# A four-layer network of attention and mixtures on one core: 24 blocks of 32 gathered slots in place of dense experts

## The reference, cut to what matters

```python
logits = einsum('btc,ce->bte', x, Wg)
probs = softmax(logits)
top_vals, top_idx = top_k(probs, 2)
gates = (one_hot(top_idx, E) * top_vals[..., None]).sum(-2)
h = relu(einsum('btc,ech->bteh', x, W1) + b1)
y = einsum('bteh,ehc->btec', h, W2) + b2
out = einsum('bte,btec->btc', gates, y)
```

## Time and profile before

| | |
|---|---|
| median of 3 runs | 462.35 us (462.15 to 462.73) |
| span of the profiled execution | 461.0 us |
| PE busy | 438.0 us, 95% |
| DVE busy | 333.3 us, 72% |
| ACT busy | 232.7 us, 50% |
| POOL busy | 139.9 us, 30% |
| moved by DMA | 62.38 MB |

### The profile page before, as it was taken

One profiled execution on the slowest core, in us unless ns is written; L12 is line 12 of the kernel. 1 busy time (PEld: TensorE's weight loads), 2 busy tenths in 40 slices (PEclk: granted clock), 3 DMA queues, 4 the chain that ended last, 5 costly groups with the idle time before them and its releaser, 6 DMA issues.

```text
span 461.0 us, 9333 instructions
## 1 busy us (share of the span) xinstructions
PE 438.0 (95%) x3240; PEld 380.5 (83%) x3240; DVE 333.3 (72%) x756; ACT 232.7 (50%) x596; POOL 139.9 (30%) x178
## 2 busy tenths in 40 slices
PE   8999999999999999999999978899899999999997
PEld 7776999997676899998577756657699999879997
DVE  3775989995576989996475486511698999787774
ACT  1494455641295765642295275232284656365452
POOL 6012556561011465652001101200445665400000
PEclk9999999999999999999999999999999999999999
DMA  5560264710480155620389606005053756326650
GB/s 161 203 204 2 77 227 138 214 64 2 155 297 2 70 183 177 202 89 1 105 231 297 154 1 175 33 20 222 0 173 135 222 158 217 121 71 191 195 202 19
DMA packets 19365, 62.38 MB, mean 135 GB/s; under 512 B 4041, under 2 KB 6914, under 8 KB 19330
## 3 DMA queue, kind: packets, MB, share of 16 engines
q1 hardware_dynamic: 19330, 61.93, 42.5%
HBM read 59.82 MB, written 2.10 MB: 134 GB/s over the span
## 4 chain that ended last, share of the span: by engine, by line
PE 68%; issue 15%; ACT 6%; DVE 5%; POOL 3%; DMA 2%; POOLq 0%; SPq 0%; DVEq 0%
PE bank L1056 24%; PE bank L1064 10%; PE bank L1076 7%; ACT probs L574 5%; PE bank L724 4%; PE bank L1078 3%; PE bank L847 3%; PE bank L874 2%; PE bank L761 2%; DMA w<-in_M_w_dram 2%; PE bank L756 1%; PE bank L890 1%; POOL rstd L415 1%; PE bank L793 1%; PE bank L737 1%
## 5 line engine op out<-in xcount | busy, mean ns | idle before, releaser
L1056 PE MATMUL bank<-xT_hi,w_hi 128*128 128x256 f32 x408 | 109.2, 289 | 1.6 <-issue 1.6
L1363 DVE TENSOR_TENSOR w_lo<-w,w_hi 128x512 fp32r<-128x512 f32 x102 | 96.7, 987 | 2.3 <-ACT w_hi L613 0.4
L661 ACT ACTIVATE hid<-bank,b 128x256 f32<-128x256 f32 x150 | 62.7, 471 | 68.9 <-PE bank L1056 68.7
L1056 PE MATMUL bank<-xT_hi,w_lo 128*128 128x256 f32 x408 | 82.0, 282 | 0.0
L1056 PEld LDWEIGHTS bank<-xT_hi,w_hi 128*128 128x128 f32 x408 | 77.9, 191 | 3.9 <-issue 3.8
L471 POOL TENSOR_TENSOR w_hl<-w,consts 128x384 fp32r<-128x384 f32 x50 | 52.6, 1052 | 73.5 <-PE bank L1078 69.8
L1056 PEld LDWEIGHTS bank<-xT_hi,w_lo 128*128 128x128 f32 x408 | 63.4, 191 | 0.0
L473 POOL TENSOR_TENSOR w_hl<-w,w_hl 128x384 fp32r<-128x384 f32 x50 | 58.9, 1178 | 3.9
L1064 PE MATMUL bank<-w,hid 128*128 128x192 f32 x308 | 56.4, 327 | 2.3 <-issue 2.3
L613 ACT ACTIVATE w_hi<-w 128x512 fp32r<-128x512 f32 x102 | 58.3, 627 | 0.2 <-DMA w<-in_M_w_dram 0.2
L1056 PE MATMUL bank<-xT_lo,w_hi 128*128 128x256 f32 x204 | 57.7, 283 | 0.0
(11 more groups left out here) (178 smaller groups left out, 658.9 us busy)
## 6 DMA issues: line engine op xcount, KB each, us to landing
w<-in_M_w_dram SPq DMA_DIRECT2D x34, 768.0 KB, 5.5
w<-in_M_w_dram SPq DMA_DIRECT2D x33, 576.0 KB, 4.9
w<-in_M_w_dram SPq DMA_DIRECT2D x9, 288.0 KB, 2.8
wqkv<-in_A_wqkv_dram SPq DMA_DIRECT2D x4, 432.0 KB, 6.6
rel_scratch<-relall SPq DMA_DIRECT2D x4, 372.0 KB, 2.3
wproj<-in_A_wproj_dram SPq DMA_DIRECT2D x4, 288.0 KB, 7.4
wqkv<-in_M_w_dram SPq DMA_DIRECT2D x2, 576.0 KB, 21.1
rel<-rel_scratch SPq DMA_DIRECT2D x10, 96.0 KB
```

The costliest lines, as they stand in the source:

```text
L661: ins = act.activation(hid[:, 2 * b + c, :], bank[B_H[b]][:, c * T:(c + 1) * T], FUNC[cfg["act"]], bias=b1[:, kb, bass.ds(at, 1)])
L1056: ins = pe.matmul(bank[B_H[b]][:, c2 * T:(c2 + 1) * T], w, xs, start=(q == 0), stop=(q == 4))
L1363: dve.tensor_tensor(w1_cols(w1_lo, b), w1_cols(w1[s], b), w1_cols(w1_hi, b).bitcast(F32), ALU.subtract)\
```

## The change

**Gathering in the open mixtures.** M0, M1, M3 and M4 now gather too, in 24 blocks of 32 slots, and the four blocks of a group are four column tiles of 32. Each expert has one block of its own for its first 32 token-expert pairs: eight static blocks, two groups. What is beyond that fills 16 dynamic blocks, four groups. With 512 pairs in all, 16 blocks are enough for every routing. Which expert a dynamic block belongs to is counted on the chip (`owner`, from the number of pairs per expert). All eight experts' weights lie in SBUF (`rw1`, `rw2`). The weights of a dynamic block are copied from there to one of four tiles (`sw1`, `sw2`), at an address that depends on a register into which the expert's number was loaded (`value_load`). Tile 0 is copied by ScalarE, tile 1 by GpSimd, tiles 2 and 3 by VectorE. There is one set of tiles: w1 of the next group can be written when `up` has read the last, w2 when `down` has.

**Full precision.** The products of the experts are plain 32-bit products; the parts, and the instructions that make them, are gone. The bias b1 is a further row of w1 (K = 128 + 65). The shared experts of M3 and M4 are two further groups, ahead of the static ones, over the 128 tokens of each half. M2 runs through the same functions with four groups of two tiles of 64; its K is cut 128 + 65 in place of 96 + 96.

**What moves beside.** The attentions' weights have two slots instead of four, and their scratch tiles share memory with `sw1` and `sw2`. Experts are loaded in pairs. In A2, SyncE issues the weights of A3 behind all of M2's. At the start GpSimd also clears a part of `rw1` (64 partitions, 8 x 768 numbers each) and makes 13 small tables.

```diff
+GROUP_KINDS = (("static",) * 2 + ("dynamic",) * 4, ("static",) * 2 + ("dynamic",) * 4, ("static",) * 4,
+               ("shared",) * 2 + ("static",) * 2 + ("dynamic",) * 4, ("shared",) * 2 + ("static",) * 2 + ("dynamic",) * 4)
...
+        rw1 = sb("rw1", [P, E, KC * 768])
+        rw2 = sb("rw2", [P, E, CHUNKS * C])
+        sw1 = sb("sw1", [P, 4, KC * 768])
+        sw2 = sb("sw2", [P, 4, CHUNKS * C])
...
-                    elif n == 2:
-                        load_attn(3)
+                    if n < 3:
+                        for p in range(2 if n else 0, 4):
+                            load_w1(n, p)
+                        for p in range(4):
+                            load_w2(n, p)
...
+                        load_attn(3)
...
+            pool.memset(rw1[CR:P, :, 768:2 * 768], 0.0).then_inc(pad_ready, 1)
...
-                    pool.tensor_tensor(parts[:, :, 0], w, one, ALU.mult).then_inc(w2_hi_ready, 1)
-                    pool.wait_ge(w2_hi_ready, SB * g + b + 1)
-                    pool.tensor_tensor(parts[:, :, 1], w, parts[:, :, 0].bitcast(F32), ALU.subtract).then_inc(w2_lo_ready, 1)
+            def slot_tables():
+                for at in range(0, SLOTS - EARLY, CAP):
+                    pool.tensor_scalar(later[:, at:at + CAP], consts[:, CONST["places"]], float(32 + at), None, ALU.add)\
+                        .then_inc(tables_ready, 1)
...
+            def moe(m):
...
+                pool.wait_ge(owner_ready, OPEN[m] + 1)
+                ids = [pool.value_load(owner[0:1, 4 + g:5 + g], min_val=0, max_val=E - 1) for g in range(4)]
...
+                def w1_copy(d):
+                    if d:
+                        pool.wait_ge(hp_psum, 2 * (GROUP0[m] + SHARED[m] + STATIC_GROUPS + d))
...
+                    pool.tensor_copy(sw1[:, 1], rw1[:, bass.ds(ids[d], 1), :].rearrange("p a n -> p (a n)")).then_inc(w1c_pool, 1)
+                def w2_copy(d):
+                    if d:
+                        pool.wait_ge(yp_psum, ROUTED0[m] + STATIC_GROUPS + d)
...
+                    pool.tensor_copy(sw2[:, 1, 0:n2], rw2[:, bass.ds(ids[d], 1), 0:n2].rearrange("p a n -> p (a n)")).then_inc(w2c_pool, 1)
+                w1_copy(0)
+                pool.wait_ge(part2_ready, OPEN[m] + 1)
...
+                w2_copy(0)
+                for d in range(1, 4):
+                    w1_copy(d)
+                    w2_copy(d)
...
+                for r in range(ROUTED[m]):
+                    if r:
+                        turn_combine(r)
+                        if r + 1 < ROUTED[m]:
+                            up(sh + r + 1)
+                    turn(sh + r)
+                    if r:
+                        add(r - 1)
+                    down(sh + r)
+                add(ROUTED[m] - 1)
...
-                            dve.tensor_copy(hid_hi[:, sb2:sb2 + 2, :], hid[:, 2 * b:2 * b + 2, :]).then_inc(hid_hi_ready, 1)
...
+                    combine_turned(0)
+                    ids = [dve.value_load(owner[0:1, 8 + g:9 + g], min_val=0, max_val=E - 1) for g in range(8)]
+                    w1_copy(0, 0)
+                    dve.wait_ge(xd2_psum, 2 * OPEN[m] + 2)
+                    dve.tensor_copy(xdT[0:ROWS[1], 1, EARLY:], bank[B_XD[1]][0:ROWS[1], :]).then_inc(xd2_dve, 1)
+                    turned(0)
...
+                    w1_copy(0, 1)
+                    group_out(0)
+                    combine_turned(1)
+                    w2_copy(0, 0)
+                    w2_copy(0, 1)
...
+                    for r in range(1, ROUTED[m]):
+                        d = r + 2 - STATIC_GROUPS
+                        if d < 4:
+                            w1_copy(d, 0)
+                        turned(r)
...
+                        if d < 4:
+                            w1_copy(d, 1)
+                        group_out(r)
+                        if r + 1 < ROUTED[m]:
+                            combine_turned(r + 1)
+                        if 1 <= d - 1 < 4:
+                            w2_copy(d - 1, 0)
+                            w2_copy(d - 1, 1)
```

More of the change, by code:

```diff
@@ L690, in _, with turned @@
-            k = 0
-            for kind, n in BLOCKS:
-                if kind == "moe" and n != 2:
-                    for b in range(HB):
-                        split(n, 0, 0, b)
+                def turned(g):
+                    at = GROUP0[m] + g
+                    for b in range(2 if g < sh and not glu else 1):
+                        act.wait_ge(hT_psum, 2 * at + b + 1 if not glu else 2 * GROUP0[4] + g + 1)
+                        act.activation(hT[:, b * 384:(b + 1) * 384], bank[B_HT[b]][:, 0:384], ACT.Copy).then_inc(hT_act, 1)
@@ new lines, in moe @@
+                act.wait_ge(xd_psum, 2 * m + 1)
+                slots = 2 * T if cfg["cap"] else T
+                if cfg["cap"]:
+                    act.activation(xdT[:, 0, 0:slots], bank[B_XD[0]][:, 0:slots], ACT.Copy, scale=lnm[:, 0:1]).then_inc(xd_act, 1)
+                    hidden(0)
+                    for g in range(len(GROUP_KINDS[m])):
+                        turned(g)
+                        if g + 1 < len(GROUP_KINDS[m]):
+                            hidden(g + 1)
+                    return
@@ new lines, in moe @@
+                router()
+                if sh:
+                    up(0)
+                    positions()
+                    up(1)
+                    static_tokens()
+                    first_blocks()
+                    for g in range(sh):
+                        turn(g)
+                        down(g)
+                else:
+                    stay_warm(5)
+                    positions()
+                    stay_warm(2)
+                    static_tokens()
+                    if not cfg["cap"]:
+                        first_blocks()
@@ L1509, in moe @@
-                for e in range(2 * looped(m), cfg["n"]):
-                    hidden(e // 2, e % 2, last=e == cfg["n"] - 1)
-                    add(e // 2, e % 2, last=e == cfg["n"] - 1)
-                dve.wait_ge(acc_done, 2 * BASE[m + 1])
+                    if not cap:
+                        then(dve.scalar_tensor_tensor(g2[:, :], csum[:, :], 1.0, rden[:, :], ALU.subtract, ALU.mult))
+                        then(dve.scalar_tensor_tensor(g21[:, :], csum[:, :], 2.0, rden[:, :], ALU.subtract, ALU.mult))
@@ L1514, in _ @@
+                settle()
+                last = m == len(MOE) - 1
+                for t in range(TT):
+                    dve.wait_ge(sum_psum, m + 1)
+                    ins = dve.tensor_tensor(x[:, t, :], bank[B_SUM][:, t * C:(t + 1) * C], x[:, t, :], ALU.add)
+                    if last:
+                        ins.then_inc(acc_done, 1)
+                    else:
+                        then(ins)
+                at = [own[0] - 1, own[0]]
+                return at
             dve.memset(warm[:, :], 1.0).then_inc(warm_ready, 1)
+            then(dve.memset(xn[:, :, C:], 1.0))
```

1176 lines of the change are left out of this document (624 added, 552 removed).

## The result

The changed kernel takes 497.58 us in the median of five runs, the kernel before 462.63: 7.4% more (ratio 1.0739, 95% interval 1.0722 to 1.0756). The five runs lie between 496.31 and 507.85, where those of the kernel before stay within 0.7 us; the profiled one, with a span of 506.0, is one of the two long ones, and the ratio is from the other three, whose mean granted clock (0.943 to 0.945 against 0.929) makes 54 to 56 us at half clock where the profiled one has 72.

The account below looks back on a forecast made before the run. TensorE bounds the kernel, busy 95% at full clock. Open mixtures +1.7 (12 us gained and lost to waits in M0 and M1), A0 +1.0, A3 +0.5: 464.2 span, 465.6 us median; range 448 to 486.

Parts of the forecast that it names:

- M0's head: Start of M0, from rstd: 10.2 us, from M2's 10.8 less half the dispatch, plus 0.4 for counting blocks.
- Rival (c): Clock falls to 1.2 GHz in waits, slowing the up behind: about 487 us for eight falls, 476 for four; chance 0.12.
- thirteen waits of 2 to 4 us: TensorE waits in the open mixtures: nine of about 3 us in M0, M1, M3, four of 2 to 4 in M4.
- 6 us of dense work stand between the waits: Open mixtures: the reason given against the clock falling in the waits; 6 us of dense TensorE work separates them.
- Up(4) and up(5): Fifth and sixth group's up wait for GpSimd's w2 then w1 copy: 3.1 us each, 2.8 in M4.
- the middle of down(0): First group's down waits for turned hidden values behind VectorE's eight register loads: 3.0 us.
- down(1): Second group's down waits for VectorE's backlog of copies and combine products: 1.4 us.
- M4's up(3): Fourth group's up in M4 waits for VectorE's backlog: 2.1 us.
- The load's price: Register load of an expert number: 0.43 us plus two checks of 0.05, 0.53 in all.
- which covers most of the 7.75: A0: GpSimd's 5.32 us idle covers most of its memset (5.1) and tables (2.65), leaving +1.0 us.
- four tiles side by side: Four column tiles of 32 run at once, so a group costs what M2's does: up 2.7 us.
- copies that exclude each other: GpSimd and VectorE copies in the open mixtures take turns, full exclusion: 0.5 us more at up(4) and up(5).

Follow-up runs that it names:

- The version with all four moves: Changed kernel with GpSimd copying w1 before w2, VectorE's register loads earlier, padding cleared in pieces within A0, bias rows turned in A0's last third: 436.87 us.
- the pair: The version with all four moves, plus TensorE register loads (idle, 492.42 us) or constant products (busy, 456.75 us) ahead of up(4) and up(5) in open mixtures.
- two such moves: Changed kernel with only the padding cleared later, within A0's softmax: 502.38 us; with only the bias rows turned earlier, in A0's last third: 502.19 us.
- the last idle kernel: The version with all four moves, plus eight TensorE register loads ahead of up(4) and up(5) of each open mixture: 492.42 us.

## Why the prediction was wrong, step by step

The version with all four moves has the same products at full clock. So PE's busy time in a stage, less that of the same stage there, is what half clock cost in the profiled execution of the change, and the rest can be held against the forecast:

| stage | forecast | measured | half clock | rest |
|---|---|---|---|---|
| A0 | 39.8 | 46.65 | 39.90 - 37.49 = 2.4 | 44.2 |
| M0 | 66.0 | 78.75 | 62.48 - 54.03 = 8.5 | 70.3 |
| M1 | 65.9 | 72.40 | 60.47 - 54.10 = 6.4 | 66.0 |
| M2 | 39.4 | 41.54 | 0 | 41.5 |
| M3 | 72.7 | 81.15 | 68.31 - 61.61 = 6.7 | 74.5 |
| M4 | 63.8 | 68.96 | 53.86 - 48.76 = 5.1 | 63.9 |

Of the 41.8 us between the forecast span (464.2) and the measured one, 29 are the clock, 4.4 A0, 4.3 M0's head, 2.1 M2 and 1.8 M3; 0.2 is spread over the others. For the median, 10 us below, the clock's part is about 22, an estimate from 54 to 56 us of half clock at the same price.

**The clock was the step that failed.** Rival (c) named the mechanism and where it would act, and had a chance of 0.12. It was set up as a rival to the forecast's waits, though it is their consequence: who forecasts thirteen waits of 2 to 4 us has to price what such a wait does to the clock. The reason against it, "6 us of dense work stand between the waits", holds nothing: of the thirteen waits twelve came, and nine of them were followed by a fall, as were the two that the forecast did not have, in A0 and at M0's head. That the kernel before never shows a fall was no evidence, since it never waits. Its price was also off: 2.7 us a fall was meant, and at the pair it is 25 us over eight waits, 3.1 each; behind the shorter idle times in the kernel before 1.5 to 1.6. The Trainium skill, "TensorE: Matmul & The Clock Gate", Part 1, says that a gate halves the clock of an engine that was little used; the rows at 0.50 agree, and the forecast cited the page and gave it too little weight.

**The waits themselves were right.** Up(4) and up(5) wait 3.01 each in M0, M1 and M3 (3.1 forecast) and 2.2 in M4 (2.8); the middle of down(0) 3.3 to 3.7 (3.0). Two waits did not come: down(1) (1.4 forecast) and M4's up(3) (2.1). In the profiled run the ups ahead of them are slow, 3.98 us in M0 and 5.34 in M4, and cover them; with the waits filled and the clock full they are about 0.5 and 0.7. Without half clock M1 and M4 come out within 0.2 us of the sum, but that is in part luck: their waits are some 1.6 and 1.8 us shorter than forecast, and the rest of the stage is longer by as much.

**The load's price** was mis-sized: 5.15 us for eight is 0.64 each, checks included, against 0.53 taken. A load's own record on VectorE is 0.30:

```profile
L1665 DVEq TENSOR_LOAD <-owner x32: 296/298/545, 74.2 to 463.2; - x32
L1665 DVEq FUSED_REGOPS  x32: 183/183/206, 74.8 to 463.5; - x32
```

The Trainium skill's floor of about 600 ns for the load alone ("DMA: Bandwidth & Descriptors", Latency and other measured facts) does not agree with this record, which is half of it. It is nearer to the 0.64 of a load with its checks than the forecast's 0.53 from SyncE's issue, but not for its own reason.

**A0** failed at "which covers most of the 7.75". That looked at GpSimd's own queue alone. The prediction had just argued from the earlier trace rows that GpSimd and VectorE take turns, and did not ask which step of VectorE the 5.2 us memset would hold. The timeline of VectorE and GpSimd in A0 of the changed kernel:

```profile
9.40 5.27 DVE L1348 TENSOR_SCALAR sw<-bqkv 128x192 f32<-128x192 f32 x1 [2.66 <-DMA wproj<-in_A_wproj_dram]
...
9.34 5.21 POOL L510 MEMSET rw<- 64x6144 f32 x1
```

VectorE's scaling of a bias, 0.26 us otherwise, starts 0.06 us behind the memset and ends 0.12 behind its end; TensorE waits 5.07 us. In the kernel with filled waits it started just ahead of the memset:

```profile
9.17 0.26 DVE L1356 TENSOR_SCALAR sw<-bqkv 128x192 f32<-128x192 f32 x1 [2.42 <-DMA wproj<-in_A_wproj_dram]
9.35 0.86 DVE L1359 TENSOR_SCALAR sw<-bank,bq_col 96x256 f32<-96x256 f32 x2
...
9.28 5.31 POOL L510 MEMSET rw<- 64x6144 f32 x1
```

There A0 is 42.99 us, and TensorE waits 3.0 for the rel copies instead, behind the tables (4.5 us for 13, not 2.65). A tenth of a microsecond decides which of the two it is.

**M0's head** was taken from M2's, and a transfer was left out: the bias rows go to main memory and back before the first up. The timeline of M0's head:

```profile
58.99 0.73 ACTq L736 DMA_DIRECT2D rw<-b_rows  x1
...
65.24 3.43 PE L1172 MATMUL bank<-rw,qT 128*32 128x384 f32 x20 [4.81 <-issue]
65.29 1.47 POOL L581 COPY sw<-rw 128x1536 f32 x1 [3.63 <-DMA rw<-b_rows]
```

ScalarE issues the way back at 58.99, and up and GpSimd's first copy both start as it lands, 6.3 us later. The change section lists the bias as "a further row of w1"; the prediction priced the row's products and not its way there.

**M2** was put at 0 by its equal columns. It also got the transposed gates per group: four times 0.36 to 0.44 on TensorE, twice with a wait of 0.5 for VectorE's copy of them, where the kernel before turned all of them at once in 1.09. That is about 1.5 of the +2.1, and the longer way to the first up (11.1 us for 10.8) 0.3.

**Right by their steps:** the groups' own products (an up of 2.79, a down of 2.16 where the forecast has 2.7 and 2.0 from the earlier trace rows), four tiles side by side, copies that exclude each other (GpSimd's w1 copy takes 1.46 alone and 2.0 to 2.3 beside VectorE's, VectorE's w2 copy 0.8 and up to 2.0), A3's weights, which came 0.3 us late (QKV waits 0.70 for them; 0.5 was forecast).

## What to carry to other kernels

A forecast wait on TensorE has two prices, its own length and what the clock makes of the work behind it; where nothing in the old trace waits, the old trace says nothing of the second, and a stretch of its own that waits, or a short test, has to. Fill a wait with products or remove it, but don't judge the removal of one wait by the total while others of its size are left: here two such moves gave nothing alone and 8 us together with the rest. And when two engines take turns, follow every long instruction of the one through the other's queue, not only through its own.

## What the runs showed of the hardware

- Idle times of TensorE of 1.8 to 5.1 us were followed by half clock in most cases, not in all: eleven of fourteen in the change, two of three in the kernel before with idle time added, all eight of the last idle kernel. The shortest, 1.8 us, is in M0 of the kernel whose padding is cleared later. The clock stayed low for 3 to 10 us each time.
- In kernels with the same waits the falls come at different ones of them, and the runs of such a kernel differ by 2 to 14 us; the versions without such waits repeat within 1.5 us. One execution of each kernel was profiled, so where the falls came in the other runs is not shown.
- A scaling on VectorE from SBUF to SBUF (TENSOR_SCALAR, 0.26 us alone) lasted to the end of a GpSimd memset that was under way, 5.27 us. VectorE's step out of PSUM (0.86 us for two, at 9.35 in the last A0 rows) went on beside the same memset, and so did two sums of two SBUF tiles each (TENSOR_TENSOR `sw<-x,bproj`, 0.61 us at 13.35, as long as without the memset).
